# Looping the convolution of the second layer, and moving the first splits of its recurrent stage

## The reference

```python
h = relu(einsum('ts,bsh->bth', adj, x @ Wg0 + bg0))
h = relu(einsum('ts,bsh->bth', adj, h @ Wg1 + bg1))
for p in range(1, MAX_SKIP + 1):
    nw = Tv // p
    wins = h[:, :nw * p, :].reshape(Bv * nw, p, Hd)
    last = _lstm_last(Wih[p - 1], Whh[p - 1], bih[p - 1], bhh[p - 1], wins)
    idx = jnp.arange(nw) * p + (p - 1)
    h = h.at[:, idx, :].set(last.reshape(Bv, nw, Hd))
return h
```

## Time and profile before

| | |
|---|---|
| median of 3 runs | 2192.06 us (2190.82 to 2192.34) |
| the profiled execution | 2191.07 us |
| its span, first to last instruction | 2188.7 us |
| PE busy | 2109.0 us (96%) |
| PE's weight loads | 1846.2 us |
| DVE busy | 1374.2 us (63%) |
| ACT busy | 1156.4 us (53%) |
| POOL busy | 473.9 us (22%) |
| mean granted clock of PE | 0.988 |

### The profile page before, as it was taken

The page is one execution under the profiler, slowest core; times in us unless marked ns, Lnnn a source line. Parts: engine busy times, 40 slices in busy tenths (PEclk is TensorE's granted clock), DMA queues, the critical chain, the costliest instruction groups (busy, mean ns, idle before and its releaser), DMA issues. The chain is left out here.

```text
span 2188.7 us, 43823 instructions
## 1 busy us (share of the span) xinstructions
PE 2109.0 (96%) x17941; PEld 1846.2 (84%) x17941; DVE 1374.2 (63%) x2736; ACT 1156.4 (53%) x2184; POOL 473.9 (22%) x1132
## 2 busy tenths in 40 slices
PE   6999999999989989999999999999999999899998
PEld 4999899989989978888888999988888799777886
DVE  5788888888876644433334444354443588876775
ACT  1554455455543467644444444353443477657987
POOL 3446654665450000000000000000000122003343
PEclk9999999999999999999999999999999999999999
DMA  4001111111122110000000000000000143001333
GB/s 124 21 21 54 55 31 40 54 55 31 50 89 92 41 52 20 1 20 1 0 1 20 20 1 1 1 1 20 1 1 1 49 128 116 1 20 47 81 88 78
DMA packets 77095, 83.32 MB, mean 38 GB/s; under 512 B 7136, under 2 KB 74592, under 8 KB 76000
## 3 DMA queue, kind: packets, MB, share of 16 engines
q1 hardware_dynamic: 76896, 80.53, 12.2%
HBM read 55.34 MB, written 25.17 MB: 37 GB/s over the span
## 5 line engine op out<-in xcount | busy, mean ns | idle before, releaser
L332 PE MATMUL ps<-R 128*128 128x256 f32 (+3 forms) x8136 | 1492.3, 343 | 13.7 <-DVE R L1494 8.0
L332 PEld LDWEIGHTS ps<-R 128*128 128x128 f32 x8136 | 1309.9, 190 | 171.4 <-issue 9.0
L1440 ACT ACTIVATE late_half<-ps,lstm_bias 128x512 f32<-128x512 f32 (+2 forms) x460 | 283.0, 669 | 375.9 <-PE ps L332 375.9
L374 POOL TENSOR_TENSOR ln_veps<-ln_mv,eps_tile 128x2 f32<-128x2 f32 x128 | 26.7, 209 | 1176.5 <-DVE ln_mv L357 1176.5
L301 POOL TENSOR_TENSOR H<-H 128x128 f32<-128x128 f32 x384 | 203.5, 562 | 10.0 <-DVE H L919 8.7
L1510 DVE TENSOR_TENSOR late_half<-late_half 128x1024 f32<-128x1024 f32 (+2 forms) x32 | 37.6, 1176 | 183.8 <-ACT late_half L1440 183.8
L1434 ACT ACTIVATE late_half<-late_half 128x1024 f32<-128x1024 f32 (+2 forms) x66 | 68.1, 1032 | 124.6 <-DVE late_half L1515 78.5
L1007 PE MATMUL ps<-H 128*128 128x256 f32 x512 | 125.4, 389 | 0.8 <-ACT H L720 0.8
L1512 DVE TENSOR_TENSOR late_half<-late_half 128x1024 f32<-128x1024 f32 (+2 forms) x32 | 37.6, 1176 | 131.1 <-ACT late_half L1440 131.1
L1031 PE MATMUL ps<-H 128*128 128x256 f32 x512 | 118.0, 381 | 0.0
L400 DVE SCALAR_TENSOR_TENSOR H<-H,ln_rstd 128x256 f32<-128x256 f32 x192 | 101.4, 568 | 15.5 <-POOL ln_rstd L367 13.3
(11 more groups left out here) (213 smaller groups left out, 2553.5 us busy)
## 6 DMA issues: line engine op xcount, KB each, us to landing
H<-in_x SPq DMA_DIRECT2D x64, 256.0 KB, 2.9
residual<-H SPq DMA_DIRECT2D x32, 256.0 KB, 2.2
H<-residual SPq DMA_DIRECT2D x32, 256.0 KB, 3.7
arena<-residual SPq DMA_DIRECT2D x32, 256.0 KB, 2.7
residual<-arena SPq DMA_DIRECT2D x32, 256.0 KB, 2.1
H_state<-residual SPq DMA_DIRECT2D x32, 256.0 KB, 2.9
out<-H_state SPq DMA_DIRECT2D x64, 128.0 KB, 2.4
arena<-in_wih SPq DMA_DIRECT2D x4, 1024.0 KB, 4.9
```

What stands on the lines that cost most here:

```text
L332: mm = pe.matmul(out, lhsT(a), rhs(b), start=start and n == 0, stop=stop and n == len(PASSES) - 1)
L1440: ins = act.activation(into[q][:, m, 0:x.cols], gate_ps(q, m, x.cols), ACT.Tanh if q == TANH_G else ACT.Sigmoid, bias=lstm_bias[:, x.p - 1 ...
```

## The change

Layer 1's convolution becomes a loop on the chip (`Fori`) on each engine that takes part: on PE the body is FIRST, SECOND and MIX_OUT of a turn and MIX_IN of the next, for turns 1 to 6, with turn 7 written out; on ACT and DVE the body is a turn, for turns 1 to 5, with 6 and 7 written out; on SP the reloads. Waits and addresses in the bodies are worked out from a register. MIX_IN of turn 1 becomes a fifth woven slot on PE (NEXT_IN). ACT's evictions of turn 0 move ahead of most of slot 18 (MIX_OUT at tick 141, formerly 212). ACT's and SP's waits for all of `y_stored` come ahead of their loops. The split of the recurrent stage's first weights goes to turn 6, the split of its first stream's first input to turn 7; after the barrier ACT and DVE only add to the semaphores that PE waits for. For this the split rows h1 are kept in the buffers of zg (`fm`), and the input's halves in `begun_x`. All ticks of `plan0` are new: the order that results is nearly the old one on PE, ACT and DVE within layer 0, while on POOL slot 16 comes ahead of slots 17 and 11, and slot 13 later.

```diff
-    MIX_IN, FIRST, SECOND, MIX_OUT = 200, 201, 202, 203
+    MIX_IN, FIRST, SECOND, MIX_OUT, NEXT_IN = 200, 201, 202, 203, 204
...
-    h1 = [Wq_r, Wk_r, Wv_r, w0r(2, KD, GROUP)]
+    begun_x = [W1_r[:, 1], w0r(KD, COLS)]
+    h1 = fm
...
-        pe={0: 12, 1: 20, 3: 30, 4: 35, 5: 40, 6: 45, 9: 58, 10: 61, 11: 66, 13: 76, 14: 83, 15: 89, 150: 90, MIX_IN: 99, FIRST: 113, SECOND: 140, MIX_OUT: 156},
-        act={0: 17, 3: 32, 4: 37, 5: 41, 7: 52, 9: 58, 10: 63, 13: 75, 14: 85, 18: 167, 140: 86, MIX_IN: 101, FIRST: 122, MIX_OUT: 212},
-        dve={1: 26, 2: 28, 3: 35, 6: 49, 8: 58, 11: 71, 12: 73, 13: 79, 15: 97, 16: 108, 17: 154, MIX_IN: 108, FIRST: 120, SECOND: 128, MIX_OUT: 140},
-        pool={1: 15, 3: 27, 11: 59, 13: 73, 15: 85, 16: 71, 17: 150},
-        sp={2: 76, 4: 20, 18: 152, MIX_IN: 60, FIRST: 107})
+        pe={0: 11, 1: 17, 3: 28, 4: 34, 5: 37, 6: 43, 9: 55, 10: 58, 11: 63, 13: 73, 14: 80, 15: 86, 150: 87, MIX_IN: 102, FIRST: 121, SECOND: 141, MIX_OUT: 154, NEXT_IN: 174},
+        act={0: 2, 3: 21, 4: 26, 5: 32, 7: 41, 9: 47, 10: 52, 13: 64, 14: 74, 18: 157, 140: 75, MIX_IN: 94, FIRST: 118, MIX_OUT: 141},
+        dve={1: 13, 2: 17, 3: 24, 6: 37, 8: 45, 11: 60, 12: 61, 13: 68, 15: 87, 16: 95, 17: 143, MIX_IN: 101, FIRST: 119, SECOND: 121, MIX_OUT: 139},
+        pool={1: 14, 3: 18, 11: 61, 13: 82, 15: 92, 16: 43, 17: 148},
+        sp={2: 74, 4: 9, 18: 152, MIX_IN: 60, FIRST: 110})
...
-            for turn in range(2, TURNS):
+            for s in S:
+                sp.wait_ge(y_stored[s], 16 * TURNS + 16)
+            with sp.Fori(1, TURNS - 1) as turn:
                 for s in ORDER:
-                    load_rows(s, turn)
+                    sp.wait_ge(ga_done[s], turn + (ga_base + 1))
+                    sp.dma_start(xg_t[s], rows_of_group(state0, s, turn + 1)).then_inc(xg_loaded[s], 16)
...
-            for turn in range(1, TURNS):
+            for s in S:
+                act.wait_ge(y_stored[s], 16 * TURNS + 16)
+            def convolve_all(slot, turn):
+                for s in ORDER:
+                    convolve(s, slot, turn)
+
+            with act.Fori(1, TURNS - 2) as turn:
                 for slot in (MIX_IN, FIRST, MIX_OUT):
-                    for s in ORDER:
-                        convolve(s, slot, turn)
+                    convolve_all(slot, turn)
+            for turn in (TURNS - 2, TURNS - 1):
+                convolve_all(MIX_IN, turn)
+                convolve_all(FIRST, turn)
+                if turn == TURNS - 2:
+                    act.wait_ge(stage_loaded[0], 16)
+                    for k in range(KD):
+                        act.activation(wslot[k][:, 0, :], wstage[0][:, k, :], ACT.Copy).then_inc(lstm_w_hi[k], 1)
+                else:
+                    for s in (0, 1):
+                        act.wait_ge(gcn_ready[s], gcn_base + 1)
+                    act.activation(begun_x[0], Hflat[:, :, 0:COLS], ACT.Copy).then_inc(lstm_x_hi, 1)
+                convolve_all(MIX_OUT, turn)
...
+            with dve.Fori(1, TURNS - 2) as turn:
+                convolve_turn(turn)
+            for turn in (TURNS - 2, TURNS - 1):
+                convolve_turn(turn)
+                if turn == TURNS - 2:
+                    for k in range(KD):
+                        dve.wait_ge(lstm_w_hi[k], lstm_w_hi_base + 1)
+                        dve.tensor_tensor(wslot[k][:, 1, :], wstage[0][:, k, :], raw(wslot[k][:, 0, :]), ALU.subtract)
+                else:
+                    dve.wait_ge(lstm_x_hi, lstm_x_hi_base + 1)
+                    dve.tensor_tensor(begun_x[1], Hflat[:, :, 0:COLS], raw(begun_x[0]), ALU.subtract)
...
             weave(pe, TURNS, plan0, "pe", stage)
-            for turn in range(1, TURNS):
-                for slot in STEPS_L1:
+            with pe.Fori(1, TURNS - 1) as turn:
+                for slot in (FIRST, SECOND, MIX_OUT):
                     for s in ORDER:
                         convolve(s, slot, turn)
+                for s in ORDER:
+                    convolve(s, MIX_IN, turn + 1)
+            for slot in (FIRST, SECOND, MIX_OUT):
+                for s in ORDER:
+                    convolve(s, slot, TURNS - 1)
...
+            act.sem_inc(x_hi[0], 1)
+            act.sem_inc(w_hi, KD)
...
-            for k in range(KD):
-                split_weights(0, k)
-            for x in steps_l[0:LS]:
+            for x in steps_l[1:LS]:
                 split_x(x)
...
+            dve.sem_inc(x_ready[0], 1)
+            dve.sem_inc(w_ready, KD)
+            for x in steps_l[1:LS]:
                 split_x(x)
```

More of the change, by code:

```diff
@@ L516, in half_blocks @@
         return range(n * h, n * h + n)
-    MIX_IN, FIRST, SECOND, MIX_OUT = 200, 201, 202, 203
+    LS = 2
+    COLS = 512
+    lr = region(R[:])
+    wslot = [lr(2, GATES * D) for _ in range(6)]
+    lstm_w_hi, lstm_w_hi_base = mixed_ready, 2 * TURNS
+    lstm_x_hi, lstm_x_hi_base = atT_ready[0], TURNS
+    MIX_IN, FIRST, SECOND, MIX_OUT, NEXT_IN = 200, 201, 202, 203, 204
     ORDER = (3, 2, 1, 0)
@@ L764, in convolve @@
                 if slot == MIX_IN:
-                    act.wait_ge(ga_done[s], ga_base + turn + 1)
+                    act.wait_ge(ga_done[s], turn + (ga_base + 1))
                     act.activation(graph_order(zg[s][:, 0]), mixed_by_graph(s), ACT.Copy).then_inc(zg_hi[s], 1)
                 if slot == FIRST:
-                    act.wait_ge(tg_ready[s], tg_base + KD * turn + KD)
+                    act.wait_ge(tg_ready[s], KD * turn + (tg_base + KD))
                     act.activation(h1[s][:, 0], tg_f[s], ACT.Relu).then_inc(h1_hi[s], 1)
                 if slot == MIX_OUT:
[L771 to L774, removed]
+                    act.wait_ge(gb_done[s], turn + (gb_base + 1))
                     for k in range(KD):
@@ L881, in add_mixed_bias @@
             def add_mixed_bias(s, turn):
-                dve.wait_ge(g0_done[s], g0_base + turn + 1)
+                dve.wait_ge(g0_done[s], turn + (g0_base + 1))
                 for k in range(KD):
@@ L957, in _, with convolve_turn @@
             weave(dve, TURNS, plan0, "dve", stage)
-            for turn in range(1, TURNS):
+            def convolve_turn(turn):
                 for s in ORDER:
@@ L1119, in stage @@
                 if opening(slot) and turn == TURNS - 1:
-                    convolve(s, slot, 0)
+                    if slot == NEXT_IN:
+                        convolve(s, MIX_IN, 1)
+                    else:
+                        convolve(s, slot, 0)
             def convolve(s, slot, turn):
                 if slot == MIX_IN:
-                    pe.wait_ge(xg_loaded[s], xg_base + 16 * turn + 16)
-                    if turn:
-                        pe.wait_ge(gcn_ready[s], gcn_base + turn)
+                    pe.wait_ge(xg_loaded[s], 16 * turn + (xg_base + 16))
+                    if first(turn):
+                        pe.wait_ge(var2_ready[s], 2 * TURNS + 1)
                     else:
-                        pe.wait_ge(var2_ready[s], 2 * TURNS + 1)
+                        pe.wait_ge(gcn_ready[s], turn + gcn_base)
                     mix_by_graph(pe, s, xg_t[s], adjT).then_inc(ga_done[s], 1)
                 if slot == FIRST:
-                    if turn == 0:
+                    if first(turn):
                         pe.wait_ge(wg_ready, wg_count)
-                    pe.wait_ge(zg_ready[s], zg_base + turn + 1)
+                    pe.wait_ge(zg_ready[s], turn + (zg_base + 1))
                     for m in range(KD):
@@ L1140, in convolve @@
                 if slot == SECOND:
-                    pe.wait_ge(h1_ready[s], h1_base + turn + 1)
+                    pe.wait_ge(h1_ready[s], turn + (h1_base + 1))
                     for n in range(TILES):
@@ L1148, in convolve @@
                 if slot == MIX_OUT:
-                    pe.wait_ge(ug_ready[s], ug_base + turn + 1)
+                    pe.wait_ge(ug_ready[s], turn + (ug_base + 1))
                     mix_by_graph(pe, s, ug_t[s], adjT).then_inc(gb_done[s], 1)
             weave(pe, TURNS, plan0, "pe", stage)
-            for turn in range(1, TURNS):
-                for slot in STEPS_L1:
+            with pe.Fori(1, TURNS - 1) as turn:
+                for slot in (FIRST, SECOND, MIX_OUT):
                     for s in ORDER:
                         convolve(s, slot, turn)
+                for s in ORDER:
[3 more added lines that the diff above has]
+                    convolve(s, slot, TURNS - 1)
     end_phase()
-    LS = 2
-    COLS = 512
     SHORT_STEP_AT = 8
@@ L1585, in _ @@
                             w = wslot[SLOTS[name, x.p - 1][k]]
+                            parts = begun_x if n == 0 else [x.operand(src[s][:, h]) for h in range(2)]
                             mm = exact_mm(pe, gate_ps(q, m, x.cols), lambda h: w[:, h, f],
-                                          lambda h: x.operand(src[s][:, h])[:, k, :], a == 0, a == len(operands) - 1)
```

(1 more changed line is left out.)

13 lines of the change are left out of this document (4 added, 9 removed).

## The result

| | before | after |
|---|---|---|
| median | 2192.11 us (4 runs) | 2179.10 us (4 runs, 2177.37 to 2180.21) |
| ratio to before | | 0.9942, 95% interval 0.9928 to 0.9956 |
| the profiled execution | 2191.07 us | 2180.21 us |
| its span | 2188.7 us | 2177.6 us |
| six turns of the convolution, from the first FIRST to the seventh | 102.56 us | 99.26 us |

The change makes the kernel 0.6% faster, where I had forecast 0.6% slower. The first rival, blocks that stay held, had forecast 2181.5.

What follows compares the result with a forecast made beforehand. The prediction took TensorE (PE), busy 96% of the span, as the bound. Its terms +1.0 + 13.0 + 5.0 + 0.5 - 6.0 = +13.5 us gave 2205 us (own range 2195 to 2219), overall range 2179 to 2216.

Steps and rivals of the forecast that it cites:

- B: Convolution as a loop: five jumps back each need an instruction fetch, +13.0 us, plus +5.0 for the clock, +0.5 for registers.
- +13.0 us for jumps: PE's convolution loop: five of six turns begin with a 3.5 us fetch, of which 0.5 and 0.4 us are hidden.
- +5.0 for the clock: PE's convolution loop: idle time at the jumps may lower the clock, taken as 1.0 us per jump.
- the stalls "within each turn": Convolution turns on PE: issue stalls, mean 1.03 us, stay; counted at nothing, 0 to 0.5 us per turn either way.
- The registers' +0.5: Loops on ACT, DVE and SP: register arithmetic not hidden between PE's last mixing out and FIRST, between 0 and 3 us.
- A: Layer 0 into the loop: FIRST gains 1.1 us, but waits for stores and meets the low clock; +1.0 us, -1 to +3.
- C: Recurrent stage's start: earlier splits let PE start 4.7 us sooner, the clock gives -1.3; -6.0 us, between -7.3 and -4.
- The clock's -1.3: Recurrent stage's start: PE idles 3.3 us instead of 8.0, so the clock may stay up; between 0.7 and 2.5 us won.
- D: Remaining parts, with layer 0's order and POOL's: counted at nothing, gain at most the 4.1 us of PE's idle time.
- rival 3: Layer 0: POOL's slot 16 ahead of a reciprocal DVE needs costs 1 us per turn, 8 us on top, 2213; chance 0.06.
- Rival 1: PE's convolution loop: blocks stay held, turns 2 to 6 run without fetches, -5.1 us; 2181.5, range 2177 to 2187; chance 0.34.
- Rival 2: PE's convolution loop: jumps miss but are mostly hidden, 5 x 1 us, no clock falls; 2192, no difference; chance 0.08.

Runs made afterwards that it cites:

- pe_body_3: The changed kernel with three turns in the body of PE's convolution loop (two passes, about 2150 instructions); 2192.22 us, ratio 1.0004.
- pe_body_2: The changed kernel with two turns in the body of PE's convolution loop (three passes, about 1430 instructions); 2181.89 us, ratio 0.9958.
- act_wait_late: The changed kernel with ACT's wait for `y_stored` moved from ahead of its loop to ahead of turn 6; 2174.72 us, ratio 0.9920.
- before_pe_loop: The kernel before with only PE's turns 1 to 7 of the convolution as a loop, waits worked out from a register; 2183.95 us, ratio 0.9966.

## Why the prediction was wrong

**The step that failed (B):** "By this picture the loop's head, three blocks back, is gone when PE jumps to it". I had read from rows 8 to 10 how far ahead PE asks, one block, and taken it for how much it keeps. The first says nothing on the second: PE keeps at least 5.6 blocks. So +13.0 us for jumps and +5.0 for the clock were nothing, and the stalls "within each turn", counted as staying, went after the first pass, since nothing is fetched any more. From turn 2's FIRST to turn 7's it is 80.73 us (670.39 to 751.12), formerly 85.01 (rows 3 and 4: 672.81 to 757.82): -4.3 us. Written out again the loop's part is +4.8 us by the runs (4.4 in the trace); put alone into before it is -5.5 us in the trace's six turns, -7.5 by the ratio. The registers' +0.5 is at most 16.17 - 16.06 = 0.1 us a turn.

The two terms would also have been too small had the jumps missed: pe_body_3's jump costs 6.8 us, less the 0.5 us wait for DVE, where I had 3.6 for a jump with its clock. That a stall of 1.46 us never lowered the clock held in before's trace only: 1.59 us did in pe_body_2.

**A, right in kind, two sizes off that cancel.** FIRST waited for ACT's split, ACT for a store, PE stood still and the clock fell, as forecast. ACT's last L385 ended at 646.45, not 650.4: 3.1 us of that are layer 0's gain, the rest the new order at its end. The landing took 4.04 us by ACT's wait, not 2.2. FIRST started at 651.86 instead of 654.1. The clock cost 1.1 us (13.08 less 11.96), forecast 1.6 to 2.3; the first pass's stall is 0.2 us shorter. In all turn 1 gained 2.4 us, and without layer 0's 3.1 part A is +0.7, where I had +1.0. What I did not draw from it: the wait costs 4.4 us by the runs, and ACT doesn't need it there. SP's own wait holds back turn 2's rows, and with them all that follows turn 1, until the stores have landed; act_wait_late leaves that one in place.

**C, right, and 1.8 us too high.** -4.2 us in the trace (17.57 less 21.80) for -4.7 of idle time, since the barrier takes 3.77 us rather than 3.3. The clock's -1.3 did not come: even 3.77 us of idle time lowered it, and it rose only 5.7 us after PE had started, as before. 

**D, wrong in size.** "Gain at most the 4.1 us of idle" was right and "at nothing" was not: turn 7's first mixing came 3.1 us sooner, 2.9 of it gained behind 70 us, by POOL's line and PE's. I had looked only for what POOL's order might hold up (rival 3, refuted by after, whose PE waits for nothing in layer 0), not for what it held up already: PE never waited for POOL, but it waited for DVE and ACT, and one of these for POOL.

**The sum:** +0.7 - 4.3 - 4.2 - 3.1 = -10.9 us, which is what the recurrent stage's first matmul gained (768.69 for 779.62); the span gained 11.1. Rival 1 had the mechanism, but its 2181.5 came so close by luck: its -5.1 and -6.0 were too high by 2.6 together, and layer 0's 3.1 was missing. **Rival 2** (hidden misses) falls with the first: nothing missed.

**The chances.** Two figures named in the prediction stood for rival 1, no row against it, and still the forecast had 0.52. Where capacity is unknown and the sum turns on it by 23 us, the two cases deserved even chances. The measured 2179.1 lies at the very low end of my range, where only rival 1 had put any weight.

## What to carry to other kernels

A loop on the chip can save time as well as code: once its body is held, the instruction fetches go, and with them the stalls of stretches with many short matmuls; on PE bodies of up to 5.6 blocks of 256 instructions were held, and one of 8.4 was not. A wait for stores belongs ahead of the first instruction that needs it, not at the nearest place outside the loop. When the steps of a plan are moved, follow who waits for whom over two engines. Here POOL's line and PE's each gave their part of layer 0's gain alone (1.3 and 1.7 of 2.9 us), but PE's line without the others' lost more than that at the end of layer 0. And compare two traces from a mark behind the start-up: a fall of the clock at 44 us that one of them has and the other hasn't was as large as the effect looked for.

## What the runs showed of the hardware

- PE asks for one block ahead (worked out from rows 9 and 10), but keeps far more: bodies of 2.8 and 5.6 blocks run from what is held (127 and 130 packets), one of 8.4 does not (143).
- A jump to a held block costs at most 0.24 to 0.28 us. The one missed jump of pe_body_3 cost 4.3 us of idle time, more than the 3.5 us estimated for a sequential fetch, and the clock's 2.5 us behind it.
- Near 686 us an idle time of 1.59 us in pe_body_2 was followed by a spell at 1.2 GHz (FIRST 13.26 us), and one of 1.87 us in pe_body_3 as well (0.61 and 0.54 in 688 to 692 us); at 747.63 us one of 1.88 us in pe_body_3 was not (FIRST 11.77 us). In layer 0 1.17 us was followed by a low clock in before_pe_loop (0.50 in 266 to 268 us) and not in before (1.00), and 4.12 us at 40 to 44 us by a low clock in after and not in before. The length of the last idle time alone does not decide.
- Stores of 256 KB landed in 2.2 us before and in 3.8 us after. In after the last two went out at 645 to 647 us, one directly behind the other, and the first load of 1 MB at 647 to 649; the loads of turn 2's rows went out only behind them, from 650 us. But before's last store went out at 651 us, as its first load of 1 MB did, and landed in 2.3 us. What lengthened them was not tried.
